# Eight transpositions of a fused attention and MLP block moved from the head of a step to the visit behind the attention output

## The reference

```python
h = layernorm(x) * (1 + ca) + sa
x = x + ga * attn(h)
h = layernorm(x) * (1 + cb) + sb
x = x + gb * ffn(h)
```

```python
v_new = A @ v - (A @ wk) @ S
o = rk_g @ S + intra @ v_new
S = gamma_C * S + wk_g @ v_new
return h + (alpha * o) @ Wr.T
```

## Time and profile before

| | us |
|---|---|
| median of 3 runs (lowest to highest) | 1745.33 (1743.48 to 1747.3) |
| span of the profiled execution | 1742.3 |
| PE matmul busy | 1716.0 (98%) |
| DVE busy | 1115.4 (64%) |
| ACT busy | 963.3 (55%) |
| POOL busy | 593.5 (34%) |

### The profile page before, as it was taken

The page is one execution under the profiler, slowest core; times in us unless marked ns, Lnnn a source line. Parts: engine busy times, 40 slices in busy tenths (PEclk is TensorE's granted clock), DMA queues, the critical chain, the costliest instruction groups (busy, mean ns, idle before and its releaser), DMA issues.

```text
span 1742.3 us, 60528 instructions
## 1 busy us (share of the span) xinstructions
PE 1716.0 (98%) x25488; PEld 1651.6 (95%) x25488; DVE 1115.4 (64%) x3041; ACT 963.3 (55%) x2249; POOL 593.5 (34%) x694
## 2 busy tenths in 40 slices
PE   8799999999999999999999999999999999999999
PEld 5698999999999999999999999999999999999998
DVE  5677666666666666676666676666666666666432
ACT  4664555555555555555555555555555555565554
POOL 3544333343333343333243333243233243243101
PEclk8899999999999999999999999999999999999999
DMA  8101000000000000000000000000000000000000
GB/s 291 68 14 33 12 23 23 18 20 11 24 23 23 18 20 11 24 23 24 17 21 15 20 23 23 20 17 19 16 23 23 21 17 21 14 23 17 8 3 12
DMA packets 37356, 47.08 MB, mean 27 GB/s; under 512 B 9236, under 2 KB 29336, under 8 KB 37080
## 3 DMA queue, kind: packets, MB, share of 16 engines
q1 hardware_dynamic: 35088, 40.75, 8.4%
q10 hardware_dynamic: 1992, 2.38, 0.5%
HBM read 22.53 MB, written 8.39 MB: 18 GB/s over the span
## 4 chain that ended last, share of the span: by engine, by line
PE 93%; DVE 1%; issue 1%; POOL 1%; ACT 1%; DVEq 0%; POOLq 0%
PE mlp L1163 64%; PE mlp L1235 6%; PE solo L1163 3%; PE duo L1431 3%; PE solo L1304 3%; PE solo L1136 2%; PE duo L1352 1%; PE duo L1129 1%; PE duo L1420 1%; PE solo L1440 1%; PE duo L1124 1%; PE duo L1325 1%; PE solo L1146 1%; PE duo L1422 1%; PE duo L1316 1%
## 5 line engine op out<-in xcount | busy, mean ns | idle before, releaser
L1163 PE MATMUL mlp<-act_hi,w_hi 128*128 128x256 f32 x4096 | 968.0, 283 | 1.1 <-POOL act_lo L668 0.6
L1163 PE MATMUL mlp<-act_lo,w_hi 128*128 128x256 f32 x4096 | 945.2, 277 | 0.0
L1163 PEld LDWEIGHTS mlp<-act_hi,w_hi 128*128 128x128 f32 x4096 | 770.1, 188 | 9.8 <-POOL act_lo L668 1.3
L1163 PEld LDWEIGHTS mlp<-act_lo,w_hi 128*128 128x128 f32 x4096 | 770.4, 188 | 0.8
L805 ACT ACTIVATE full<-mlp,scale_sb 128x256 f32<-128x256 f32 x512 | 246.4, 481 | 553.7 <-PE mlp L1163 553.5
L895 DVE TENSOR_TENSOR act_lo<-full,act_hi 128x256 fp32r<-128x256 f32 x512 | 240.2, 469 | 321.7 <-ACT act_hi L806 319.1
L668 POOL TENSOR_TENSOR act_lo<-full,act_hi 128x256 fp32r<-128x256 f32 x256 | 186.6, 735 | 501.9 <-ACT act_hi L795 501.9
L806 ACT ACTIVATE act_hi<-mlp,scale_sb 128x256 fp32r<-128x256 f32 x512 | 242.6, 474 | 0.0
L1163 PE MATMUL mlp<-xh,w_hi 128*128 128x256 f32 x768 | 190.8, 286 | 3.5 <-issue 3.0
L1163 PE MATMUL mlp<-xl,w_hi 128*128 128x256 f32 x768 | 189.8, 282 | 0.0
L607 POOL TENSOR_TENSOR rstd<-ve,minus_half 128x2 f32<-128x2 f32 x64 | 49.1, 768 | 331.7 <-DVE ve L844 331.3
(11 more groups left out here) (179 smaller groups left out, 2679.9 us busy)
## 6 DMA issues: line engine op xcount, KB each, us to landing
w_raw<-in_wts SPq DMA_DIRECT2D x22, 512.0 KB, 5.0
kg<-r SPq DMA_DIRECT2D x64, 126.0 KB
xin<-in_x SPq DMA_DIRECT2D x62, 128.0 KB
out_y<-y SPq DMA_DIRECT2D x62, 128.0 KB, 2.5
step_and_inv<-square_t SPq DMA_DIRECT2D x56, 64.0 KB, 2.0
wmod_sb<-in_wmod ACTq DMA_DIRECT2D x1, 1024.0 KB, 9.1
kg<-last SPq DMA_DIRECT2D x64, 2.0 KB
last<-r SPq DMA_DIRECT2D x64, 2.0 KB, 1.7
```

Source lines behind the costliest of these rows:

```text
L1163: mm = pe.matmul(dst, *general_ops, start=is_first and i == 0, stop=is_last and i == 1)
```

## The change

The item `start` of `mixed` moves. Before, it is the second item of a step, with ahead 1, between column 7 of `l2` (the last item of the step before) and column 0 of `l3`. After, it stands in the step before that with ahead 2, behind `attn_out` and in front of column 7 of `l2`. For the first steady step it has to be issued by the warm-up, so `third` gets it as its last item. Nothing else is changed.

```diff
-    mixed = listed([("rg", 0, 0), ("start", 0, 1)], late + layers[:2 * HK], {
+    mixed = listed([("rg", 0, 0)], late + layers[:2 * HK], {
         ("l3", 0): [("norm2", 0, 0)],
...
         ("l2", 5): [("unit", 0, 2)],
-        ("l2", 6): [("attn_out", 0, 0), ("residual", 0, 2)],
+        ("l2", 6): [("attn_out", 0, 0), ("start", 0, 2), ("residual", 0, 2)],
     })
...
         ("l2", 5): [("n", 2, 1), ("unit", 0, 2)],
-        ("l2", 7): [("n", 3, 1)],
+        ("l2", 7): [("n", 3, 1), ("start", 0, 2)],
     })
```

## The result

The changed kernel takes 1777.39 us in the median (1775.27 to 1780.46, 4 runs), the kernel before 1745.06 us (1743.48 to 1747.3, 4 runs). The ratio is 1.0184, with a 95% interval of 1.0169 to 1.02: 32 us slower. The forecast was 1775.5 us.

A forecast was written before the change was run, and what follows sets the result against it. PE, busy 98% of the span, was taken as the bound; 27 moved visits at 1.12 us each add 30.2 to 1745.3, giving 1775.5 us. The range was 1743.5 to 1779.5.

The forecast's parts named there:

- PE's own work: Merged visit on PE: 8 transpositions stay 8, last matmul of `l2 7` at offset 4.33; saves about 0.04 a step.
- GpSimd ahead of DVE: In moved steps GpSimd's L647 starts at 5.50, DVE's L895 at 5.52 and waits; chance 0.62, range 1772 to 1780.
- DVE first: Rival: L647 starts no earlier than L895, so no wait; 1.1 gained in all, 1744.2; chance 0.20.
- The price: `l3 0`: `act_lo` ends at 7.07, 15th matmul at 7.22 against 6.10; 1.12 a step, 30.2 over 27 steps.
- The restart of PE: PE's weight load and start after `act_lo` ends, taken as 0.15 with a bound of 0.05.
- The gain of the merged visit: Attention output and transpositions in one PE visit: 0.04 a step, 1.1 in all if nothing waits.
- The cover of 0.1: Slack between `act_lo` ready (5.94) and the 15th matmul of `l3 0` (6.06); falls from 1.0, still enough.
- the estimate by the full 0.42: L895 runs its whole 0.42 only after L647: 1.26 a step, 34.0 in all, 1779.3.
- A changed pace of matmuls: Example given for something else slower on PE; no size, chance 0.03.

The follow-up runs named there:

- e2: Changed kernel plus a two-column GpSimd multiply into an unread tile right in front of `base` in steady steps; ratio 1.0025 to the kernel before.
- e1: Changed kernel plus a wait: in steady steps GpSimd starts `base` only when `act_lo` of column 7 of `l2` is done; 1.0000, 1748.77 us against 1747.82.
- e3: Changed kernel with `base`'s first instruction (512 columns) written as two halves of 256; ratio 1.0103 to the kernel before.
- e7: Changed kernel with `base`'s first instruction written as four quarters of 128 columns; ratio 1.0085 to the kernel before.
- e6: Changed kernel with the merged visit's parts in the other order, transpositions and then attention output; ratio 1.008 to the kernel before, 1761.49 us.
- e8: Changed kernel with both `base` instructions on 2 of 256 columns in steady steps, so the output is incomplete; ratio 1.0044 to the kernel before, 1755.06 us.
- e4: Changed kernel with DVE's two `rT` copies moved behind `act_lo` of column 7 of `l2`; ratio 1.0176 to the kernel before.
- e5: Kernel before with the transpositions' visit moved behind column 0 of `l3` instead of ahead of it; ratio 1.0019, 1751.18 us against 1747.48.
- e9: Kernel before with `residual` listed ahead of `attn_out`, changing GpSimd's order alone so `base` comes before `rstd`; ratio 1.0009.
- e10: Changed kernel with `residual` listed ahead of `attn_out` and `start` still last; ratio 1.0094 to the kernel before.

## Why the prediction was right

**PE's own work.** The last matmul of `l2 7` was expected at offset 4.33 and is at 4.33 (969.01). Step 1 of the warm-up was a true picture of the merged visit.

**GpSimd ahead of DVE.** `rstd` was expected at 0.70, L647 at 5.50 and L895 at 5.52. They are at 0.69, 5.50 and 5.52, and the order is the same in all 27 steps. The forecast rested on a margin of 0.02 that had been put together from rows of two steps; the offsets repeat to 0.01 from step to step, which is why that was enough. The rival (DVE first) differed by that alone, so the reading was sound but the sign had some luck in it: in the one step with halves the same margin moved by 0.03 and DVE was first. e2 shows the other side of it.

**The price.** `act_lo` was expected to end at 7.07 and ends at 7.04. The restart of PE was taken as 0.15 and then a matmul every 0.115. In fact the 15th matmul starts 0.06 after `act_lo`'s end and the 16th 0.22 later, so the 16th is at 7.32 against 6.21: 1.11, where the sum had 1.12. That it fits so closely is luck in part: the end of `act_lo` was put 0.03 and the restart 0.09 too late, and the 0.11 by which PE's next matmul is late was not in the sum. A step grew from 52.00 to 53.12. 27 x 1.12 = 30.2 was the sum. The span grew by 31.1, of which 30.9 are in the 27 steps: some of them, in both kernels, are longer by single pauses of up to 0.7. The median grew by 32.3, and runs of one kernel lie 4 to 5 us apart, so what is left over the sum can't be told from their scatter.

**The gain of the merged visit.** 0.04 a step was expected if nothing waits. That isn't borne out. In e1 `act_lo` isn't held up and ends at 5.93, and an undisturbed step takes 52.02, no less than before. The cover of 0.1 was counted to the 15th matmul, but the weights of this matmul are loaded before it; in the kernel before, their load starts 0.11 ahead of it (953.07). In e1 it starts 0.06 after `act_lo`'s end, as in the changed kernel, and 0.19 after the load before it in place of 0.11, so PE is held back by about what the visit gains:

```profile
538.46 0.19 PEld L1150 LDWEIGHTS mlp<-act_lo,w_hi 128*128 128x128 f32 x1
538.65 0.19 PEld L1150 LDWEIGHTS mlp<-act_hi,w_hi 128*128 128x128 f32 x1
```

In e2 `act_lo` ends at 5.97 and a step takes 52.03. The rival "DVE first" was therefore priced too low by some 0.06 to 0.07 a step, 2 us, and by the pace of PE (below) too low again.

**The rule of the Trainium skill.** The Trainium skill, "SBUF — State Buffer", section "SBUF: two separate sides", has whoever starts first hold the pair for a whole instruction. The runs agree on who waits (e2, and one step of e3, turn it round) and on one instruction as the unit (e3, e7). They don't bear out that the whole of L880 runs only after GpSimd's end: it alone takes 0.42, but it ends 0.28 after that. The rows decide, and the estimate by the full 0.42, 1779, was too high.

**What was left without a price.** A changed pace of matmuls stands in the prediction with a chance of 0.03 and no size. It didn't come in the changed kernel, but in the profiled runs of e1, e6, e7 and e8, at 0.6 a step, more than the merged visit might have given. None of the versions beats the kernel before; e1, which has the change and no collision, is level with it (1.0000).

## What to carry to other kernels

A visit of small matmuls between two layers is also cover for the chain of the last column (two activations and a subtraction, 1.6 us here, behind 14 matmuls that last 1.6 us). Before moving it, work out when that chain ends and what else runs on the port of each of its instructions at that time. When two engines share a port, compare starts, not shares of busy time: 0.02 us decided over 32 us, and a wait (e1) or a tiny instruction (e2, which is left 4 us slower) on the less urgent engine settles it. And look in the warm-up or the tail of the trace: the order that one wants to try may already be there once.

## What was not expected of the hardware

**A shorter power.** `rstd` on 2 columns takes 0.80 to 0.90 when an `act_lo` subtraction is running on DVE as it starts, and 0.69 to 0.73 in every other case, over all its instructions in the twelve profiled runs. Had it kept its 0.83 in the changed kernel, `base` would have started at 5.63 by the prediction's rows, behind `act_lo`, and the loss would not have come; that is an estimate.

**Small SBUF copies wait as well.** L918 copies 8 columns within SBUF and takes 0.17, but 1.25 to 1.27 behind a `base` instruction of GpSimd (80 of the 81 steady steps of e4, e5 and e9). L919, from PSUM, takes its 0.68 beside a running GpSimd instruction (in e5 it starts at 1065.52, and L654 runs from 1065.54 in its usual 1.18).

**PE has two paces.** Matmuls of columns 2 to 7 of `l3` follow each other every 0.113 us in some steps and every 0.118 in others, at a granted clock of 1.00 both times. A step with the slower pace is 0.5 to 0.6 longer. Two stretches of 9 us at the same place of two steps of e1 (the columns are stretch, length, PE busy and matmuls, PEld, DVE, ACT, POOL, clock, DMA share, GB/s):

```profile
492.00:501.00 9.00, 9.00 (x79) 9.00 (x78) 7.07 (x29) 4.14 (x12) 2.54 (x4) 1.00 0.12 34
544.66:553.66 9.00, 9.00 (x82) 9.00 (x81) 7.09 (x30) 4.48 (x13) 2.48 (x4) 1.00 0.12 34
```

The step with 79 matmuls there takes 52.66, the one with 82 takes 52.02. In e8 the same two counts are found, with hardly a DMA in those stretches:

```profile
493.56:502.56 9.00, 9.00 (x79) 9.00 (x78) 7.09 (x29) 4.11 (x11) 2.58 (x4) 1.00 0.01 2
...
598.49:607.49 9.00, 9.00 (x82) 9.00 (x81) 7.10 (x30) 4.45 (x13) 2.52 (x4) 1.00 0.01 3
```

The kernel before has 82 in the same stretches of four steps in a row, and 23 of its 27 steady steps are within 0.06 of the shortest; in e1 it is 9 of 27.

By the starts of the matmuls, the slower pace is there in this many of the 27 steps of the profiled runs: 16 in e1, 13 in e6, 12 in e8, 9 in e7, 2 in e3, 1 in e4, and none before, in the changed kernel, e2, e5, e9 and e10. So it isn't bound to whether PE waits for `act_lo`: in e7, e3 and e4 PE waits and it comes, in e2 and e5 PE doesn't wait in the steady steps, but for one of e2, and it stays away. A count holds for one execution only. That of e1 is the slowest of twelve (1755.66, where the median is 1748.77 and the lowest 1745.96), and the kernel before was profiled once. Neither DMA nor the clock tells the two apart. What sets the pace was not found, and no run was made for it; it is left open.
